# The last convolution of a deformable convolution: two half images in one pass of 256 columns

## The reference, cut to what matters

```python
sampled = v00*(1-wy_)*(1-wx_) + v01*(1-wy_)*wx_ + v10*wy_*(1-wx_) + v11*wy_*wx_
sampled = sampled * mask[:, :, None]          # (image, group, channel, tap, row, col)
wr = w.reshape(C_out, DG, Cg, P)              # P = 9 taps
out = jnp.einsum('bgcphw,ogcp->bohw', sampled, wr) + b[None, :, None, None]
mu = out.mean(axis=(0, 2, 3), keepdims=True)
var = out.var(axis=(0, 2, 3), keepdims=True)
```

## Time and profile before

| what | us |
|---|---|
| median of 3 runs | 129.36 (129.3 to 129.49) |
| profiled execution: span from first to last instruction | 127.3 |
| median less that span | 2.06 |
| sampling loop, first transpose to the end of the last convolution | 65.6 to 105.1 |

### The profile page before, as it was taken

The page is one execution under the profiler, slowest core; times in us unless marked ns, Lnnn a source line. Parts: engine busy times, 40 slices in busy tenths (PEclk is TensorE's granted clock), DMA queues, the critical chain, the costliest instruction groups (busy, mean ns, idle before and its releaser), DMA issues.

```text
span 127.3 us, 3032 instructions
## 1 busy us (share of the span) xinstructions
PE 114.2 (90%) x1200; PEld 82.3 (65%) x1201; DVE 74.4 (58%) x149; ACT 68.3 (54%) x121; POOL 25.9 (20%) x34
## 2 busy tenths in 40 slices
PE   6989889998989899997977899999999987989990
PEld 5667566577423325877966678888888975656750
DVE  0076976718984362129999599699493004346241
ACT  4254796357630407027978959969956631347000
POOL 8996000004940000002616050050000000000000
PEclk9999999999999999999999999999999999999997
DMA  3544000000101000000000000000000000000002
GB/s 106 168 56 110 12 0 5 0 1 8 34 0 31 3 17 14 5 5 0 0 0 5 0 0 5 0 0 5 0 8 0 0 8 0 0 0 0 5 0 88
DMA packets 3060, 2.22 MB, mean 17 GB/s; under 512 B 1570, under 2 KB 2754, under 8 KB 3040
## 3 DMA queue, kind: packets, MB, share of 16 engines
q0 software_dynamic: 464, 0.67, 2.7%
q1 hardware_dynamic: 2144, 0.74, 2.4%
q10 hardware_dynamic: 432, 0.55, 1.2%
HBM read 1.68 MB, written 0.26 MB: 15 GB/s over the span
## 4 chain that ended last, share of the span: by engine, by line
PE 59%; DVE 21%; ACT 12%; issue 6%; DVEq 0%; ACTq 0%
PE ps L977 9%; PE ps L489 5%; DVE smat L913 5%; PE ps L991 5%; PE ps L1001 4%; PE ps L1293 4%; PE ps L514 3%; PE ps L496 3%; PE ps L276 3%; PE ps L287 3%; ACT tx L848 2%; DVE smatT L740 2%; PE ps L518 2%; PE ps L655 2%; ACT rstd L530 2%
## 5 line engine op out<-in xcount | busy, mean ns | idle before, releaser
L913 DVE TENSOR_TENSOR smat<-ty,tx 128x1536 f32<-128x1536 f32 (+1 forms) x14 | 21.5, 1555 | 4.3 <-ACT tx L848 4.2
L954 ACT ACTIVATE smatT<-ps 128x1536 f32<-128x1536 f32 x12 | 17.4, 1450 | 7.8 <-PE ps L977 7.6
L977 PE MATMUL ps<-cst,smat 128*128 128x128 f32 x144 | 18.1, 275 | 2.6 <-DVE smat L913 2.3
L977 PEld LDWEIGHTS ps<-cst,smat 128*128 128x128 f32 x144 | 15.7, 140 | 4.3 <-DVE smat L913 3.2
L489 PE MATMUL ps<-cst 128*128 128x256 f32 x48 | 13.0, 387 | 0.3 <-issue 0.3
L1001 PE MATMUL ps<-samp,wc 128*128 128x128 f32 x72 | 11.0, 291 | 0.0
L991 PE MATMUL ps<-smatT,xt 128*32 128x96 f32 x384 | 10.4, 249 | 0.4 <-ACT samp L945 0.4
L1001 PEld LDWEIGHTS ps<-samp,wc 128*128 128x128 f32 x72 | 8.9, 191 | 1.6
L489 PEld LDWEIGHTS ps<-cst 128*128 128x128 f32 x48 | 8.3, 190 | 2.2 <-issue 1.3
L830 POOL TENSOR_SCALAR disty<-disty 128x288 f32<-128x288 f32 x3 | 6.2, 2081 | 17.2 <-ACT disty L837 17.2
L991 PEld LDWEIGHTS ps<-smatT,xt 128*32 128x32 f32 x384 | 7.9, 109 | 2.3 <-issue 1.8
(11 more groups left out here) (200 smaller groups left out, 198.1 us busy)
## 6 DMA issues: line engine op xcount, KB each, us to landing
cst<-in_cst ACTq DMA_DIRECT2D x1, 278.0 KB, 3.5
x<-in_x SPq DMA_DIRECT2D x2, 128.0 KB, 2.9
ew<-in_L_ffn_weight POOLq DMA_DIRECT2D x4, 64.0 KB, 2.2
ew<-in_L_ffn_weight POOLq DMA_DIRECT2D x1, 256.0 KB, 4.2
w<-in_L_ffn_ffn_w SPq DMA_DIRECT2D x3, 64.0 KB
cst<-in_cst ACTq DMA_DIRECT2D x1, 129.0 KB, 3.0
out<-fin SPq DMA_DIRECT2D x1, 128.0 KB, 2.2
out<-fin ACTq DMA_DIRECT2D x1, 128.0 KB, 2.1
```

The source lines that it names most:

```text
L913: return nc.vector.tensor_tensor(smat[:, n % 3, BP * part.start:BP * part.stop, :].rearrange("p u (g r c) -> p (u g) r c", g=DG, c=W), ty[ ...
L954: nc.scalar.activation(smatT[:, n % 2, :, :, :].rearrange("p k g n -> p (k g n)"), ps[:, bank:bank + 3, :].rearrange("p b n -> p (b n)"), ...
L977: last = nc.tensor.transpose(ps[:, bank + u // BP, (u % BP) * P:(u % BP + 1) * P], smat[:, n % 3, u, :], ident)
```

## The change

All twelve steps get a home of their own in `samp`, arranged so that the two halves of an image stand side by side for each tap. One matmul per tap then takes both halves, 256 columns. A pair of steps (same image, same ki) is convolved when both of its halves are sampled: the six pairs follow the products of steps 4, 6, 7, 10 and 11, and the sixth comes at the end. The wait of a sample copy for the convolution of two steps before goes. The wide branch, which is not run here, convolves all pairs at its end.

```diff
-        samp = sb("samp", [P, 2, K3, P])
+        samp = sb("samp", [P, J * K, K3, NH, P])
...
+        PAIR_AFTER = (4, 6, 7, 10, 11)
+
+        def sampled(q):
+
+            jh, ki = q // K, q % K
+            return samp[:, jh // NH * K + ki, :, jh % NH, :]
+
+        def convolve_pair(q):
+
+            j, ki = q // K, q % K
+            for kk in range(K3):
+                tap = K3 * ki + kk
+                last = nc.tensor.matmul(ps[:, 7, j * N:(j + 1) * N], wc[:, tap, :, :].rearrange("p g o -> p (g o)"),
+                                        samp[:, q, kk, :, :].rearrange("p h n -> p (h n)"),
+                                        start=(tap == 0), stop=(tap == TAPS - 1))
+            return last
+
...
             def keep(q):
                 act.wait_ge(sem("f_mm"), q + 1)
-                if q >= 2:
-                    act.wait_ge(sem("f_cv"), q - 1)
-                nc.scalar.activation(samp[:, q % 2, :, :], ps[:, 6, 0:K3 * P], ACT.Copy).then_inc(sem("f_samp"), 1)
+                nc.scalar.activation(sampled(q), ps[:, 6, 0:K3 * P].rearrange("p (k n) -> p k n", k=K3),
+                                     ACT.Copy).then_inc(sem("f_samp"), 1)
...
             def convolve(q):
-                jh, ki = q // K, q % K
-                pe.wait_ge(sem("f_samp"), q + 1)
-                for kk in range(K3):
-                    tap = K3 * ki + kk
-                    last = nc.tensor.matmul(ps[:, 7, jh * P:(jh + 1) * P], wc[:, tap, :, :].rearrange("p g o -> p (g o)"),
-                                            samp[:, q % 2, kk, :], start=(tap == 0), stop=(tap == TAPS - 1))
-                last.then_inc(sem("c_out" if q == NSTEP - 1 else "f_cv"), 1)
+
+                pe.wait_ge(sem("f_samp"), K * (NH * (q // K) + NH - 1) + q % K + 1)
+                return convolve_pair(q)
...
                 products(n)
-                if n:
-                    convolve(n - 1)
-            convolve(NSTEP - 1)
+                if n in PAIR_AFTER:
+                    convolve(PAIR_AFTER.index(n))
+            convolve(J * K - 1).then_inc(sem("c_out"), 1)
```

More of the change, by code:

```diff
@@ L1033, in keep @@
                 dve.wait_ge(sem("w_mm"), WGROUP * (q + 1))
-                if q >= 2:
-                    dve.wait_ge(sem("w_cv"), q - 1)
-                nc.vector.tensor_copy(samp[:, q % 2, :, :], ps[:, 6, 0:K3 * P]).then_inc(sem("w_samp"), 1)
+                nc.vector.tensor_copy(sampled(q), ps[:, 6, 0:K3 * P].rearrange("p (k n) -> p k n", k=K3)
+                                      ).then_inc(sem("w_samp"), 1)
             for n, (jh, ki, g, w_) in enumerate(WIDE):
@@ L1118, in products @@
                 last.then_inc(sem("w_mm"), 1)
[L1120 to L1127, removed]
             transposes(0)
@@ L1133, in wide_pe @@
                 if n and n % WGROUP == 0:
-                    convolve(n // WGROUP - 1)
+                    pe.wait_ge(sem("w_samp"), n // WGROUP)
                 products(n)
-            convolve(len(WIDE) // WGROUP - 1)
+            pe.wait_ge(sem("w_samp"), NSTEP)
+            for q in range(J * K):
+                last = convolve_pair(q)
+            last.then_inc(sem("c_out"), 1)
         @block.sync
```

## The result

The changed kernel takes 130.38 us (median of 4 runs, 130.01 to 130.78) where the kernel before takes 129.33 (median of 4, 129.21 to 129.49): a ratio of 1.008, 95% interval 1.0045 to 1.0116. It is slower by 1.05 us, with the forecast at 130.1 and its range at 129.5 to 130.8. The profiled execution has a span of 128.5 us and took 130.36.

What follows compares the result with a forecast made beforehand. A VectorE and ScalarE loop bounds the sampling stage until 86.94 us, then TensorE; there 5.3 us of convolutions become 6.8, 0.8 of the 1.5 more filling idle time. 129.36 + 0.75 = 130.1 us, range 129.5 to 130.8.

Steps and rivals of the forecast that it cites:

- Two regimes: Sampling stage: until 86.94 us a VectorE, transposes and ScalarE loop of 9.46 us sets the pace; afterwards TensorE leads almost alone.
- T(7): TensorE's twelve transposes of step 7, waiting for VectorE; start forecast unchanged at 86.94 us.
- T(9): TensorE's transposes of step 9; at 93.23 us before, after waiting for VectorE; forecast at 94.16, weights ready at 93.2.
- The price of a wide record: Convolution matmul of 256 columns: 0.214 us each against 0.112 for 128; a pair of six records 1.38 us.
- The rival that ends on the faster side: Weight load, not columns, sets the convolution's pace: 0.112 us per wide record, 127.9 us in all; chance 0.06.
- T directly behind P: TensorE step from a step's 32 products to transposes directly behind them: taken as 0.80 us, bounds 0.65 to 0.87.
- P(11): Product records of step 11 on TensorE: forecast at 102.25 us, TensorE deciding; ScalarE would allow 102.17.
- D(3): Fourth convolution pair, behind the products of step 10: forecast at 100.87 us, taking 1.38 us.
- The sum: Starts added along TensorE: clock-holding matmul after the last convolution at 105.71 instead of 104.96 us, +0.75, unchanged tail moving along.
- a falling clock: Rival: TensorE's clock sinks before the first pair at 82.6 us, about doubling times, 4.5 us more, 134.5; chance 0.03.
- Edits priced at nothing: Larger sample tile, ScalarE's copy in three runs of 128, and its removed wait on an old convolution: no cost.
- a turn: Loop of VectorE's weights, transposes, ScalarE's copies and relu before 86.94 us: 9.46 us, no convolution in it.

Runs made afterwards that it cites:

- the two half changes: Pairs for one image only, other image in single half images as before, against the kernel before: image 1 only, ratio 0.9998; image 0 only, 1.0151.
- the relu: Kernel before with one ScalarE edit: at ki = 1 the next half image's relu stands ahead of the sample copy; ratio 0.9915.
- One convolution later: Kernel before's order without pairs, the convolution of step 8 moved from behind the products of step 9 to behind those of step 10; ratio 0.9963.
- the two traces of equal order: Kernel before (18.02 us in the stage) and twelve homes plus copies in runs with the old 128-column convolution (18.03 us, ratio 0.9965).

## Why the prediction was right

- **Two regimes.** Right. T(7) stayed at 86.96 behind VectorE, and the early convolutions left only idle time; the two half changes and the relu show it from three sides. The loss itself is narrower than "behind T(7)": it lies between T(7) and T(9).
- **The price of a wide record.** Forecast 0.214 us, from the clock-holding matmuls. Measured: twelve from 103.23 to 105.92 take 2.69; less the first step of 0.31 that the prediction took, (2.69 - 0.31)/11 = 0.216. A pair takes 1.40 against 1.38. Twice the width costs 0.216/0.112 = 1.93 times as much. The rival that ends on the faster side needed less than 0.188 a record and falls with it. By the stream figures of the Trainium skill (TensorE: Matmul & The Clock Gate, "Back-to-back issue gap") it would be 1.21 times, an estimate interpolated from them; these float32 records do not bear that out.
- **T directly behind P**, the step that no row had shown: taken as 0.80, measured 95.62 to 96.42, 0.80. The prediction chose it between 0.65 and 0.87 without a row, so that it came out exactly is in part luck.
- **P(11).** Forecast at 102.25, found at 102.43. TensorE decided it, not ScalarE, whose sample copy began at 101.60; in the kernel before, P(11) came 0.63 us behind that copy (102.09 to 102.72), which would allow 102.23 here. Of the 0.18 us, 0.02 is the later T(7), about 0.05 the two pairs and the other steps ahead of D(3), and 0.11 the step from D(3) to the products: 100.94 to 102.43 is 1.49 where 1.38 was set. That is the term that was clearly too small. The weight loads ahead of those products stood idle for 0.33 us, 0.17 behind transposes:

```profile
100.14 0.65 PEld L1008 LDWEIGHTS ps<-smatT,xt 128*32 128x32 f32 x32 [0.17 <-issue]
...
101.60 0.48 ACT L961 ACTIVATE samp<-ps 128x384 f32<-128x384 f32 x1
...
102.43 0.65 PEld L1008 LDWEIGHTS ps<-smatT,xt 128*32 128x32 f32 x32 [0.33 <-issue]
```

The width is not what made the step longer. A pair takes 1.40 to a T and 1.49 to the products; twelve narrow records take 1.45 to the clock-holding matmul and 1.53 to the products (103.28 to 104.73 and 100.95 to 102.48 in *One convolution later*).

- **The sum.** Forecast +0.75 us in the stage, found 105.92 - 104.96 = 0.96, 0.02 of it in T(7)'s start; the rest is the 0.11 above and some 0.02 for each pair. The unchanged tail moved with it, as forecast (19.37 us up to the output's issue). The median moved by 1.05, with 0.45% to 1.16%, or 0.6 to 1.5 us, as its interval; that interval is wider than the 0.2% that the prediction held a measurement to tell.
- **The clock.** The granted clock stayed at 1.00, 2.4 GHz, from 65.01 to 82.66, 17.65 us with nothing but transposes and products and 4.6 us of idle time in them. The rule of the Trainium skill (TensorE: Matmul & The Clock Gate, "Part 4: PE-mode transpose") by which transposes do not count as activity the way matmuls do shows no effect here; whether the products alone keep the clock up was not tried. The price that the prediction gave a falling clock, a doubling read from the first six clock-holding matmuls, has no row at a lower clock behind it: the granted clock of the first 4 us, in which they ran, reads 1.00 too.
- **Edits priced at nothing** (homes, runs, the wait that went): nothing, 18.03 against 18.02 us in the stage.

## What to carry to other kernels

Before merging two passes into one, ask what the merged pass waits for: the first half now runs when the second is ready, and if the engine was idle at the first place and is full at the second, the whole first half is added to the time, less any idle time left at the second place (here 1.26 us less 0.29). Price a wider instruction by its step from start to start; where that grows with the width, there is little to set against the move. The same reading finds the better edit: look for the idle stretch that a movable piece can fill (one convolution behind P(10)), and for the short piece that stands in the way of a turn (0.37 us of a copy on ScalarE).

## What was not expected of the hardware

The time of a whole execution scattered by more than most of the effects here: on one of the two chips of the experiments the kernel before took between 128.92 and 130.78 us in 29 runs. The ten traces differ little in between: T(0) starts at 65.65 to 66.33 us, from the clock-holding matmul behind the last convolution to the issue of the first output transfer it is 19.36 to 19.39 us, and behind that issue 2.8 to 3.3 us are left. The stage from T(7) to that matmul agreed to 0.01 us between the two traces of equal order (18.02 and 18.03).

And the thirty-two narrow products behind a convolution begin some 0.09 us later than a T or a clock-holding matmul would, behind a wide pair (1.49 against 1.40) as behind twelve narrow records (1.53 against 1.45). Why was not tried.
